# One attention step on a Trainium2 core: the reciprocals of four softmax denominators, brought to the head's rows by column products with the identity instead of by a transpose

## The reference, cut

```python
q, k, v = proj(Wq), proj(Wk), proj(Wv)            # (4, 16, 512, 32) each
q, k = _apply_rope(q, cos, sin), _apply_rope(k, cos, sin)
scores = einsum('bhqd,bhkd->bhqk', q, k) / sqrt(32)
scores = where(causal, scores, finfo.min)
probs = softmax(scores, axis=-1)
attn = einsum('bhqk,bhkd->bhqd', probs, v)        # divided by the row's denominator
x = x + layernorm(attn @ Wo.T);  x = x + layernorm(experts(layernorm(x)))
```

## Time and profile before

| | before |
|---|---|
| median of three runs | 1165.45 us (1163.73 to 1166.33) |
| the profiled execution, its time | 1166.61 us |
| the profiled execution, its span | 1164.8 us |
| TensorE (PE) busy | 1068.5 us, 92% |
| VectorE (DVE) busy | 668.9 us, 57% |
| ScalarE (ACT) busy | 505.4 us, 43% |
| GpSimd (POOL) busy | 610.8 us, 52% |

### The profile page before, as it was taken

The page is one execution under the profiler, slowest core; times in us unless marked ns, Lnnn a source line. Parts: engine busy times, 40 slices in busy tenths (PEclk is TensorE's granted clock), DMA queues, the critical chain, the costliest instruction groups (busy, mean ns, idle before and its releaser), DMA issues.

```text
span 1164.8 us, 24407 instructions
## 1 busy us (share of the span) xinstructions
PE 1068.5 (92%) x6269; PEld 721.7 (62%) x6270; DVE 668.9 (57%) x2306; ACT 505.4 (43%) x1421; POOL 610.8 (52%) x634
## 2 busy tenths in 40 slices
PE   5999899899999979988869999999999999999954
PEld 3655566555566545655547777776777776767721
DVE  5666566556666668867644544554444444444448
ACT  3666576566666644446622222222222222222224
POOL 4434333333333313321148888887888887788810
PEclk9999999999999999989989999999999999999988
DMA  9700000000000052100169989999999999998788
GB/s 318 290 2 1 3 1 1 2 2 1 1 2 2 1 202 79 55 28 19 56 205 215 221 199 252 245 233 232 253 234 250 240 236 264 269 222 172 118 274 324
DMA packets 66279, 166.73 MB, mean 143 GB/s; under 512 B 15378, under 2 KB 17170, under 8 KB 66080
## 3 DMA queue, kind: packets, MB, share of 16 engines
q0 software_dynamic: 38496, 83.95, 33.0%
q1 hardware_dynamic: 27712, 81.88, 19.8%
HBM read 119.85 MB, written 62.65 MB: 157 GB/s over the span
## 4 chain that ended last, share of the span: by engine, by line
PE 74%; DMA 12%; DVE 6%; issue 4%; ACT 2%; POOL 1%; DVEq 0%; SPq 0%; POOLq 0%; ACTq 0%
PE ps L971 16%; PE ps L710 15%; PE ps L982 8%; PE ps L769 7%; DMA sum_rows<-x_t,idx 6%; DMA x_t<-x_rows,idx 5%; PE ps L827 4%; PE ps L955 4%; PE ps L739 4%; PE ps L789 4%; PE ps L863 2%; PE ps L724 2%; PE ps L879 2%; PE ps L843 1%; PE ps L977 1%
## 5 line engine op out<-in xcount | busy, mean ns | idle before, releaser
L971 PE MATMUL ps<-big,work 128*128 x1264 | 300.1, 380 | 0.0
L464 POOL DMA_INDIRECT sum_rows<-x_t,idx x157 | 249.9, 1592 | 55.8 <-issue 45.7
L971 PEld LDWEIGHTS ps<-big,work 128*128 128x128 f32 x1264 | 228.7, 191 | 24.8
L458 POOL DMA_INDIRECT x_t<-x_rows,idx x159 | 166.2, 1045 | 58.7 <-issue 31.7
L710 PE MATMUL ps<-big 128*128 128x384 f32 x512 | 179.2, 493 | 2.1 <-ACT big L528 1.7
L664 ACT ACTIVATE work<-ps 128x512 f32<-128x512 f32 x159 | 95.0, 597 | 188.0 <-PE ps L955 136.3
L384 POOL TENSOR_TENSOR work<-qkv_all,rope_sb 128x256 f32<-128x256 f32 x64 | 46.8, 730 | 241.9 <-ACT qkv_all L533 241.9
L982 PE MATMUL ps<-big,work 128*128 x314 | 160.9, 594 | 1.8 <-issue 1.7
L955 PEld LDWEIGHTS ps<-ident_sb,x_t 128*128 128x128 f32 x636 | 78.1, 142 | 107.4 <-issue 73.9
L1076 DVE CUSTOM_DVE_ANT_0 ps<-ps,mask_sb 128x128 f32<-128x128 f32 (+3 forms) x256 | 120.6, 513 | 24.1 <-PE ps L739 23.4
L552 ACT ACTIVATE work<-ps,neg_max 128x128 f32<-128x128 f32 (+3 forms) x256 | 132.5, 528 | 3.3 <-DVE neg_max L1076 2.4
(11 more groups left out here) (183 smaller groups left out, 1444.9 us busy)
## 6 DMA issues: line engine op xcount, KB each, us to landing
big<-experts SPq DMA_DIRECT2D x65, 768.0 KB, 14.2
sum_rows<-x_t POOLq DMA_DIRECT2D x4, 2048.0 KB
big<-sum_rows SPq DMA_DIRECT2D x8, 768.0 KB, 9.5
x_rows<-work SPq DMA_DIRECT2D x16, 256.0 KB, 2.0
sum_rows<-attn_t POOLq DMA_DIRECT2D x2, 2048.0 KB
out<-x_sb SPq DMA_DIRECT2D x16, 256.0 KB, 5.8
x_sb<-x SPq DMA_DIRECT2D x3, 1024.0 KB, 9.6
x_t<-sum_rows SPq DMA_DIRECT2D x4, 768.0 KB, 13.0
```

What stands on the lines that cost most here:

```text
L458: pool.indirect_dma_start(rows[:, q, :], None, x2_rows, bass.IndirectOffsetOnAxis(ap=idx[:, q, 0:1], axis=0), bounds_check=last_row, oob_i ...
L464: pool.indirect_dma_start(all_sums, bass.IndirectOffsetOnAxis(ap=idx[:, q, 1:2], axis=0), y_sb[:, q, :], None, bounds_check=last_sum, oob_ ...
L971: mm = pe.matmul(ps[:, 2 + p, 0:GATEUP], rows_t[:, p, c, :], w_ring[:, slot, c * GATEUP:(c + 1) * GATEUP], start=(c == 0), stop=(c == DC - 1))
```

## The change

`invert` takes the reciprocal of the four denominators alone: 128 x 4 values instead of 128 x 128. `turn_rden` becomes four products, one for each head: the weights are the head's column of reciprocals, read 32 times by a stride of zero, the moving operand is the identity, and the output is the head's 32 partitions of `rden_bank`. Semaphores, order and everything else stay.

```diff
-        rden = work[:, 2048:2176].rearrange("p (h d) -> p h d", h=HG)
+        rden = work[:, 2048:2048 + HG]
...
-                pe.transpose(rden_bank, rden[:, :, :].rearrange("p h d -> p (h d)"), ident_sb[:, :]).then_inc(s_rden_ps, 1)
+                for h in range(HG):
+                    mm = pe.matmul(rden_bank[DH * h:DH * (h + 1), :], rden[:, h:h + 1].broadcast_to([P, DH]), ident_sb[:, :],
+                                   start=True, stop=True)
+                mm.then_inc(s_rden_ps, 1)
...
-                dve.reciprocal(rden[:, :, :], den[:, :].rearrange("p (h o) -> p h o", o=1).broadcast_to([P, HG, DH])
-                               ).then_inc(s_rden, 1)
+                dve.reciprocal(rden, den[:, :]).then_inc(s_rden, 1)
```

## The result

The changed kernel takes 1194.39 us (median of six runs, 1192.94 to 1199.08), the kernel before in the same comparison 1166.69 us (1163.73 to 1169.24). The ratio is 1.0242, 95% interval 1.0220 to 1.0264: slower by 27.7 us. The prediction was 1186.2 us, with a range of 1176 to 1196: the direction and the mechanism held, the cost was put 7 us too low (20.8 us for 27.7). The profiled execution has a span of 1192.4 us against 1164.8, so 27.6 us are there to be explained.

The account below looks back on a forecast made before the run. TensorE's issue order was taken to bound the attention loop. 51 blocks x 0.40 = 20.4, block 14 0.6, last four 0.7, `norm_x` -0.9: +20.8 us, from 1165.45 to 1186.2 us, range 1176 to 1196.

Parts of the forecast that it names:

- What bounds the kernel: Attention loop: in about 60 of 64 blocks time is the sum of what TensorE issues; VectorE has slack.
- `invert`: VectorE's reciprocal in each block: from 0.944 to about 0.16 us, 50 us less work in all, nearly all landing in slack.
- The gain in block 15: Block 15 of the first three batches: TensorE's `xt` no longer waits for `norm_x`, 3 x 0.30 = -0.9 us.
- The four heads run together, and pay on entry: `turn_rden` on TensorE: four products cost 0.22 us together plus 0.13 entering 32-column weights, 0.35 us per block.
- The way back: TensorE's return from 32-column to full weights, ahead of the projection: 0.16 us per ordinary block, within its 0.40 us growth.
- Blocks 12 to 14: First three batches: the projection's wait for ScalarE's L528 hides the cost; 0, 0 and 0.21 us remain.
- The last four blocks: Blocks without projection, paced by ScalarE: the result comes 0.24 us later, passing through in three of them, +0.7 us.
- (a): Rival: passages to narrow weights and back cost nothing in `turn_rden`; +5 us, 1170.5 us; chance 0.07.
- (b): Rival: the four heads' products run one behind the other on TensorE; +62 us, 1227 us; chance 0.06.
- (c): Rival: blocks waited for VectorE's `invert`, so each gets shorter; -24 us, 1141 us; chance 0.02.
- (d): Rival: no change, the 0.40 us hides in every block as in block 12; about 1165.5 us; chance 0.03.

Follow-up runs that it names:

- VectorE's half alone: Against the kernel before: reciprocal of the four denominators, then a copy that writes each 32 times, with the old transpose kept; ratio 0.9990.
- the way back before a transpose: Against the changed kernel: the four products of `turn_rden` put ahead of head 3's transposes instead of behind them; ratio to the kernel before 1.0218.
- TensorE's half alone: Against the kernel before: four products with 32 ordinary weight columns each replace the transpose, reciprocals still written 32 times; ratio 1.0214.
- the kernel with one full product: Against the kernel before: the transpose of `rden` becomes one fp32 product of the same full 128x128 weights with the identity; ratio 1.0060.

## Why the prediction held, and where its sum was short

**What bounds the kernel: right.** Ordinary blocks are the sum of TensorE's pieces before and after, and the experiment with VectorE's half alone shows that 0.5 us less on VectorE moves none of them.

**`invert`: right.** 0.168 us against 0.16. The gain in block 15 was put at 0.30 us and measured 0.37 (6.99 to 6.62 with VectorE's half alone), probably since the weight load that was held up counts too; no run separates the two.

**The four heads run together, and pay on entry: right.** 0.35 us, as read from `weigh`.

**The way back: the mechanism right, the term too small.** I took 0.16 us from the transposes behind `weigh`, and named this as the weakest reading. Ahead of the projection it is 0.20, and the block's growth 0.44 instead of 0.40. Over 51 ordinary blocks that is 2.0 us. The sign given for it, a projection piece of 2.74 us, is 2.78. The experiment with the way back before a transpose shows it.

**Blocks 12 to 14: right.** Put at 0, 0 and 0.21 us, measured 0.00, 0.04 and 0.25, the rest being the larger way back.

**The last four blocks: too high.** Put at 0.7 us, measured 0.36 (3.97, 4.14, 5.11, 4.62 us before; 3.97, 4.36, 5.22, 4.65 after). I let the delay of ScalarE's evacuation through in three blocks, and it came through whole in one.

**Left out: the two loop edges.** The distance across an edge grew from 10.25 and 10.28 us to 11.67 and 11.55, so by 2.7 together, of which 0.9 are the block's own growth. The other 1.8 us stand beside a longer stretch at half clock, but it is not shown that all of them come from it. With TensorE's half alone, where both stretches are 3.4 us, the edges take 11.05 and 10.90 us, 1.4 more than before; so 0.5 us come without a longer stretch, and 1.3 are left for it. Part of the 0.5 may be that the products cost more at half clock: in the first block, where the clock is at half in both profiles, the piece of `turn_rden` went from 0.21 to 0.59 us, not from 0.11 to 0.35. With VectorE's half alone, whose blocks don't grow, one execution has 11.22 us where the stretch is 6.8 and 10.54 where it is 3.4. That stretch is 6.8 us in kernels without the products too and 3.4 in two with them, so it is no fixed part of their cost: it goes with whether the clock fell ahead of TensorE's first work behind the edge or after it. Why the fall came first at all four edges of the changed kernel's two profiles, and at neither with TensorE's half alone, is open.

**Left out: the start.** These are pieces of the changed kernel's chain:

```profile
2.85 7.02 DMA x_sb<-x
...
13.22 5.46 PE ps L710 x8
18.68 0.78 PE ps L700 x4
```

Of the 3.5 us ahead of the first `weigh`, 0.4 are counted as the first block's products. The other 3.1 begin with the load of `x`, 7.02 us against 5.57, and go on with the first projection, 5.46 against 4.58, and the transposes behind it, 0.78 against 0.44. Later such projections take 2.58 us; the view's granted clock for these pieces reads 1.00, so no row shows why they are up to twice as long. Over the nine profiles the first `weigh` lies between 34.9 and 38.4 us. The three earliest are the kernel before twice and VectorE's half alone (36.1); the kernel with one full product, which has no narrow products in its `turn_rden`, has 37.1. So the products are not needed for a late start, but that the two profiles of the kernel before are the earliest is not explained, and stays open.

Together: 51 x 0.44 = 22.4; block 14 and 13, three times 0.29, 0.9; block 15, three times 0.07 less the 0.44 already counted for it, -1.1; the last blocks 0.4; the edges 1.8; makes 24.4 us. The profiles show 24.0 from the first `weigh` to the last and 0.4 ahead of it. The remaining 3.1 us of the span are the start. So of the 6.8 us by which the growth of the span was put too low, 4.9 lie in the edges and the start, for which the sum had no term, and 2.0 in the way back; the small terms nearly cancel. The range held the result because it was wide enough for other misses; nothing in it was meant for the start or the edges.

**The rivals.** (a), no cost for the passages, would have shown 0.22 and 2.58 us: it shows in the kernel with one full product, which has none. (b), heads one behind the other, would have made the piece about 1.0 us: it is 0.35. (c) fell with VectorE's half alone. (d) is true of block 12 only.

No version tried beats the kernel before. The closest is VectorE's half alone, with 0.999.

## What to carry to other kernels

An instruction that is cheap for its size can still be dear for where it stands: here four narrow products cost 0.22 us of array time and 0.33 us for being between full-width neighbours, and moved next to other narrow products the second part went. Before splitting a full-width operation into column groups, look up in the chain what the existing switches of weight width cost, count the switches, and read each way back in front of the kind of instruction that will follow. And 50 us taken off an engine that waits for the bound one are worth what one row of waits says, here 1 us.

## What the runs showed of the hardware

- The way from full to 32-column weights cost 0.13 us; the way back cost 0.16 us in front of 128-column transposes and 0.20 in front of 384-column fp32 products. At such a change the weight load began together with its product, where between neighbours of one width it began 0.11 us ahead.
- From 32-column products to other 32-column products the change costs nothing: 0.35 us, then 0.22 and 0.44 for the next 8 and 16 records. That agrees with what the Trainium skill says under "TensorEngine Tiling (Array Packing)", Key Properties, that it is changing the mode that drains, not changing the tile.
- Weights read with a stride of zero load and run like ordinary ones (0.36 and 2.78 us either way).
- An fp32 product of the same size as an fp32 transpose took 0.22 us of the chain against 0.11.
- Behind a loop edge TensorE ran at half clock, 1.2 GHz, for 3.4 or for 6.8 us, in profiles of kernels whose TensorE work is the same (behind the first edge 3.4 in the kernel before, 6.8 with VectorE's half alone; behind its second edge 3.4). It was 3.4 us at the ten edges where TensorE had begun to work before the clock fell, and 6.8 at the seven where the clock fell first and at one where TensorE had begun 0.1 us before.
